# Second-layer keys of a two-layer cross-attention kernel: the layout in DRAM between the two passes

## What is computed

```python
q = (query @ Wq + bq).reshape(B, Nq, 16, 16).transpose(0, 2, 1, 3)
k = (key @ Wk + bk).reshape(B, Nk, 16, 16).transpose(0, 2, 1, 3)
v = (value @ Wv + bv).reshape(B, Nk, 16, 16).transpose(0, 2, 1, 3)
attn = softmax(einsum('bhqd,bhkd->bhqk', q, k) * SCALE)
out = einsum('bhqk,bhkd->bhqd', attn, v)
```

## Time and profile before

| | before |
|---|---|
| median of 3 runs | 1108.72 us (1107.97 to 1112.41) |
| the profiled execution, its own time | 1113.25 us |
| its span | 1111.3 us |
| busy: PE / ACT / DVE / POOL | 1073.9 / 680.0 / 635.2 / 189.3 us |
| mean granted TensorE clock | 0.991 of full speed |
| moved by DMA | 161.78 MB in 73,834 packets |
| first pass of layer two (about 618 to 822 us) | PE 95% busy, DMA 75% |
| second pass of layer two (about 833 to 1045 us) | PE 97% busy, DMA 89% |

### The profile page before, as it was taken

One profiled execution on the slowest core, in us unless ns is written; L12 is line 12 of the kernel. 1 busy time (PEld: TensorE's weight loads), 2 busy tenths in 40 slices (PEclk: granted clock), 3 DMA queues, 4 the chain that ended last, 5 costly groups with the idle time before them and its releaser, 6 DMA issues.

```text
span 1111.3 us, 29310 instructions
## 1 busy us (share of the span) xinstructions
PE 1073.9 (97%) x10316; PEld 881.9 (79%) x10316; DVE 635.2 (57%) x1068; ACT 680.0 (61%) x1198; POOL 189.3 (17%) x269
## 2 busy tenths in 40 slices
PE   9999999999999999999989999999989998999998
PEld 7887788888888888888875777777768887888873
DVE  6999544444444444444354789999984434444342
ACT  6987334343343434334331899999988897999631
POOL 0000100000000000000104667676720000000120
PEclk9999999999999999999999999999989999999998
DMA  5443700011001000100174677777768999999390
GB/s 184 141 140 117 319 30 28 28 38 28 28 28 28 28 28 30 36 28 19 66 297 150 223 253 249 241 245 244 247 207 213 231 216 202 246 241 243 93 401 6
DMA packets 73834, 161.78 MB, mean 146 GB/s; under 512 B 7697, under 2 KB 9169, under 8 KB 71633
## 3 DMA queue, kind: packets, MB, share of 16 engines
q1 hardware_dynamic: 64928, 119.06, 37.2%
q0 software_dynamic: 8880, 42.36, 10.3%
HBM read 122.57 MB, written 38.80 MB: 145 GB/s over the span
## 4 chain that ended last, share of the span: by engine, by line
PE 70%; ACT 9%; issue 8%; DVE 5%; DMA 5%; ACTq 1%; DVEq 1%; POOL 1%; SPq 0%; POOLq 0%
PE ps L773 41%; PE ps L978 8%; PE ps L1044 6%; ACT q_hk L598 6%; ACT wide L566 3%; DMA q_hk<-k_mem 3%; PE ps L830 2%; PE ps L755 1%; DMA q_le<-k_mem 1%; DVE wide L1550 1%; DVE wide L1558 1%; PE ps L834 1%; PE ps L831 1%; PE ps L833 1%; PE ps L832 1%
## 5 line engine op out<-in xcount | busy, mean ns | idle before, releaser
L1620 DVE TENSOR_TENSOR wide<-wide,probs 128x1024 f32<-128x1024 f32 x97 | 118.8, 1225 | 226.3 <-ACT probs L581 225.9
L1550 DVE TENSOR_TENSOR wide<-ps,wide 128x512 f32<-128x512 f32 (+1 forms) x194 | 184.4, 951 | 0.8 <-PE ps L773 0.8
L566 ACT CAST wide<-ps 128x512 bf16<-128x512 f32 x294 | 165.0, 609 | 11.6 <-PE ps L773 10.7
L581 ACT ACTIVATE probs<-ps 128x512 f32<-128x512 f32 x196 | 114.8, 599 | 78.8 <-PE ps L773 78.8
L773 PE MATMUL ps<-q_ha,t_ha 128*128 128x512 f32 x392 | 155.1, 396 | 1.1 <-ACT t_ha L556 1.1
L591 ACT ACTIVATE probs<-ps 128x1024 f32<-128x1024 f32 x132 | 128.3, 1025 | 26.1 <-PE ps L773 24.0
L1558 DVE TENSOR_TENSOR wide<-wide 128x512 bf16<-128x512 bf16 (+1 forms) x194 | 122.3, 630 | 19.5 <-ACT wide L566 18.9
L598 ACT ACTIVATE q_hk<-ps,wx 128x256 fp32r<-128x256 f32 x196 | 83.9, 489 | 24.8 <-PE ps L834 21.4
L576 ACT COPY weights_q<-ps 128x512 f32<-128x512 f32 x48 | 28.2, 588 | 106.2 <-PE ps L978 90.0
L773 PEld LDWEIGHTS ps<-q_ha,t_ha 128*128 128x128 f32 x392 | 74.3, 190 | 18.4 <-issue 1.5
L576 ACT COPY v_sb<-ps 128x512 f32<-128x512 f32 x50 | 29.4, 588 | 83.5 <-PE ps L773 83.5
(11 more groups left out here) (418 smaller groups left out, 2294.4 us busy)
## 6 DMA issues: line engine op xcount, KB each, us to landing
raw<-ctx_in SPq DMA_DIRECT2D x147, 256.0 KB, 2.7
k_mem<-q_hk SPq DMA_DIRECT2D x49, 512.0 KB, 3.0
v_mem<-probs SPq DMA_DIRECT2D x49, 256.0 KB, 3.4
wide<-v_mem SPq DMA_DIRECT2D x49, 256.0 KB, 5.4
q_le<-k_mem SPq DMA_DIRECT2D x34, 256.0 KB, 4.4
q_ab<-k_mem SPq DMA_DIRECT2D x32, 256.0 KB, 4.7
q_hk<-k_mem SPq DMA_DIRECT2D x32, 256.0 KB, 5.3
ring<-ex_in POOLq DMA_DIRECT2D x5, 1088.0 KB, 13.1
```

The costliest lines, as they stand in the source:

```text
L566: act.copy(half16[:, c:c + 512], ps[:, back_bank(layer, q) + u, :]).then_inc(sem(f"half{layer}"), 1)
L581: act.activation(e_keep[GT * slot + j][:, u * 512:(u + 1) * 512], ps[:, s_bank[j][u], :], ACT.Exp).then_inc(sem("exp0"), 1)
L1550: dve.tensor_tensor(r, scores, r, ALU.max).then_inc(sem(f"front{layer}"), 1)
L1620: dve.tensor_tensor(run[:, 0:1024], run[:, 0:1024], e, ALU.add).then_inc(sem("lsum"), 1)
```

## The change

The store becomes two transfers a group, one for the high part and one for the rests; each writes its 128 rows so that in DRAM the four quarters of a row of the second pass stand side by side. The load becomes one transfer of 64 rows of 8 KB for both parts. The counts waited for follow: a key store now adds 32 to `k_out`, and the load 16 to `k_in`.

```diff
@@ store_keys @@
                 sp.wait_ge(sem("k_lo"), g + 1)
-                sp.dma_start(k_mem[g].rearrange("a r n -> r a n"), ke[slot].bitcast(F32).rearrange("r (a n) -> r a n", a=2))\
-                    .then_inc(sem(f"k_out{slot}"), 16)
+                for a in range(2):
+                    sp.dma_start(k_mem[g, a].rearrange("(r u) n -> u r n", u=4), ke[slot][:, a * 512:(a + 1) * 512].bitcast(F32))\
+                        .then_inc(sem(f"k_out{slot}"), 16)
@@ load_keys @@
-                for a in range(2):
-                    rs = slice(KEYS.start + 32 * a, KEYS.start + 32 * a + 32)
-                    sp.dma_start(kp[slot][rs, :].bitcast(F32).rearrange("r (u n) -> r u n", u=4),
-                                 k_mem[g, a].rearrange("(u r) n -> r u n", u=4)).then_inc(sem(f"k_in{slot}"), 16)
+                sp.dma_start(kp[slot][KEYS, :].bitcast(F32), k_mem[g].rearrange("a (r u) n -> (a r) (u n)", u=4))\
+                    .then_inc(sem(f"k_in{slot}"), 16)
@@ SP, between the passes @@
-            sp.wait_ge(sem("k_out0"), kv_count(0, GROUPS - 1))
-            sp.wait_ge(sem("k_out1"), kv_count(1, GROUPS - 2))
+            sp.wait_ge(sem("k_out0"), 2 * kv_count(0, GROUPS - 1))
+            sp.wait_ge(sem("k_out1"), 2 * kv_count(1, GROUPS - 2))
@@ ACT, keep_keys @@
-                    act.wait_ge(sem(f"k_out{slot}"), kv_count(slot, g - 2))
+                    act.wait_ge(sem(f"k_out{slot}"), 2 * kv_count(slot, g - 2))
@@ ACT, pass2_1 @@
-                act.wait_ge(sem("k_in0"), 32)
+                act.wait_ge(sem("k_in0"), 16)
@@ DVE, keys_again @@
-                        dve.wait_ge(sem(f"k_in{slot}"), 32 * (i + 1) + (16 if slot else 0))
+                        dve.wait_ge(sem(f"k_in{slot}"), 16 * (i + 1) + (16 if slot else 0))
```

## The result

The changed kernel takes **1271.1 us** (median of 4 runs, 1269.29 to 1274.41) against 1108.35 (4 runs, 1107.8 to 1112.41): ratio **1.1453** [1.1423, 1.1483], 14.5% slower. The prediction was 1353 us, in a range of 1215 to 1425.

What follows compares the result with a forecast made beforehand. Both passes were taken as near PE's own time, the first paced by a chain through ACT and PE; +252 us for the store and -8 for the load gave +244, so 1353 us, range 1215 to 1425.

Steps and rivals of the forecast that it cites:

- The spread over four engines: First-pass key store: outermost dimension 4 in DRAM puts both transfers on the same four engines, 64 packets each a group.
- The third rival: First-pass store stays on all sixteen engines, pace stays 4.30 us; only the second pass gains, 1101 us; chance 0.12.
- The price of a packet: First-pass store: a 2 KB packet costs 128 ns, blended from 142 (narrow) and 85 (wide), giving 9.55 us a group.
- The first rival: First-pass store: four engines at 85 ns a packet, 6.8 us a group, 1221 us, or 1288 at slow PE clock; chance 0.26.
- So the queue stays filled: First pass: about 5 us from slot release to data hides under the other store's 8.2 us, so four engines set pace.
- the forecast's case: First pass at 9.55 us a group, key stores 9 to 10 us apart; roughly 1290 to 1390 us, chance 0.45.
- The loop: First pass: ACT's keys wait for the key store, landing takes 9 us or more, context loads queue behind stores.
- TensorE's clock: First pass: even at 1.2 GHz PE's 8.2 us a group would hide under 9.55, so a lower clock costs nothing.
- The second pass, -8 us: Second-pass key load: one transfer into 64 rows lands sooner than two into 32, removing late keys, -8 us.
- one of two issues less: Second-pass key load: one transfer instead of two saves an issue of 0.4 us before each landing.
- Between the passes: SP waits for the last key store, landing up to 10 us after issue, before loading: nothing, up to +5 us.
- Sum: Whole kernel: +252 us in the first pass and -8 in the second make +244 us, 1353 us.

Runs made afterwards that it cites:

- the control: The kernel before with only the next group's context load issued ahead of the two stores on SP: 1109.19 us, ratio 1.0005.
- the two pairs of loads: Kernel with the store in four 32-row transfers, its single key load made two: 32 rows of 8 KB each, 1121.6 us; 64 rows of 4 KB each, 1114.54 us.

## Why the prediction was right or wrong

**The spread over four engines: right.** The outermost 4 decides. The packet count came out to the packet, four engines without the layout lose 168 us (the 163 and the missing gain of the load), and four strips of 32 on all engines win it back but for what their four issues and the order on SP cost. The rule cited from the Trainium skill (DMA: Bandwidth & Descriptors, "Why a DMA increments its semaphore by 16 and not by 1") agrees with this trace: 54,344, and with 2 outermost 52 GB/s. The third rival, sixteen engines, falls.

**The price of a packet: wrong, and the step that failed.** "I take three parts of 142 to one of 85: 128 ns." Where the queue runs freely it is 79 to 80 ns. All told the changed kernel pays 7.6 us for 80 packets, 95 ns. The 142 came from sixteen engines that share 32 rows, and it isn't a matter of writes: sixteen engines that *read* 32 rows pay about 131 ns (the four strips). Here four engines have 128 rows between them, and the price of narrow transfers doesn't apply. The first rival's number, 85 ns, was close, but its reason, that reads in SBUF don't disturb each other, is not what the strips show. The blend treated "few rows at any moment" as narrow; the number of engines for the rows should have weighed more, as the text itself had noted ("there are four instead of sixteen to disturb each other").

By the Trainium skill (SBUF — State Buffer, "Door 1: The DMA port swizzle") rows p and p + 32 of one half of the 128 share a port, and rows 64 to 127 have other ports than rows 0 to 63. With that agree the loads (rows 32 to 95, which lie in both halves, 206 us; 32 rows at a time 217) and the slow reads of the strips; the 26 GB/s of each of two engines on rows p and p + 32 speak against it, if the two walk in step, which no run shows.

**"So the queue stays filled": right, as far as the trace shows.** Fewer than four engines are busy in 5% of the pass. But at 79 ns a group would take 6.3 us and it took 7.6: packets last longer in stretches, for which the sum had no term, and whose cause stays open. The first rival, at 85 ns with full queues, gave 6.8 us and 1221; the measured 1271 lies between its ends (1221 and 1288), but the reason given for the upper end, a slow TensorE, isn't shown: PE is busy 73% of this pass and waits. The forecast's own size, 9.55 us a group and +252 us, was 1.6 times the +159.3. "I am wrong if ... the stores start under 8 us apart" holds: the forecast's case did not occur. That the time still fell into the stated range is owed to the width that the first rival gave it, and in part to luck, since that rival's free pace (6.8 us) and the measured one (7.6) differ by something that neither foresaw.

**The loop: right in kind.** ACT's keys wait for the key store (121.6 us), landing is over 9 us (12 to 14), the context load is late behind the stores. DMA's share was to fall to about 0.4 or less and is 0.46: the same bytes in 7.6 us instead of 9.55.

**TensorE's clock, "cost nothing here": not contradicted.** It was granted 0.72 in the first pass. PE had room at that level, as argued, and I read the clock as a result of the stall. No run separates the two.

**The second pass, -8 us: right in direction, near in size.** -8.5 us from PE's first scores on, of which about 3 belong to the one profiled execution before; 6 us against the control. The waits for keys went down from 49 to 8.9 us. The reason given, that a load into 64 rows is faster than two into 32, is shown by the two pairs of loads (a share of 0.95 against 0.69 for nearly the same bytes); the 365 GB/s themselves were not read off. The part "one of two issues less" is worth nothing: two wide loads do as well as one.

**Between the passes, "nothing, up to +5 us": +4.0.** The upper end happened, since the last store is waited for until 992.12.

**Sum.** 159.3 + 4.0 - 8.5 = +154.8 against +244 foreseen. The error of 89 us is the first pass (93 us less), with 4 us between the passes the other way.

## What to carry to other kernels

When a transfer is reshaped, look at its outermost dimension on each side before its bytes: with 4 there, four engines carry it, and the mean DMA share falls while these four are the bound. Multiply their packets by the price of one from a row of the same direction, and treat it as a lower bound: here 6.3 us a group became 7.6. Take that row from a transfer with as many engines for its rows, too: sixteen engines on 32 rows paid 131 to 142 ns, four on 128 rows 79 to 95. If a layout needs such a dimension, cut the transfer there into several with 32 rows outermost, and put what others wait for ahead of them on the issuing queue; here that turned 1.145 into 0.995 to 0.997.

## What the runs showed of the hardware

- Two engines that store 32 SBUF rows each give 52 GB/s, four 98 to 107 at their best: 79 to 80 ns for 2 KB. Sixteen engines on 32 rows are slower per engine both ways: stores of strips ran at 205 to 307 GB/s with the engines 80 to 100% busy for most of it, loads into 32 rows at 205 to 238. Loading rows 32 to 95 at once instead of in two halves took DMA's share in the second pass from 0.95 to 0.69 for nearly the same bytes.
- Four engines at the same share (0.25 to 0.26) carried 57, 88 and 101 GB/s in different stretches: a busy engine isn't an engine at its best rate.
- The issue of a transfer on SP isn't a constant. The value store takes 0.35 us in one place and 1.63 in another of the same run, a context load up to 2.38 in the changed kernel, a strip on two engines 2.17 in the median and 4.3 at most. It is longest where the stores crowd few engines.
- The shape of the transfer sets the issue's least time: 0.33 us for 128 rows of 512 floats, 0.54 for 4 by 32 rows of 512.
- The same program on the same four engines ran at two paces, 7.6 and 6.4 us a group, in one execution.
